# Adding relative distances to attention scores: the strided side moved from the SBUF operand to PSUM

## The chip, the cores and the metric

One core of a Trainium2 chip runs the whole program. The metric is the device time of one execution in microseconds, the median of several runs.

## What is computed

The program runs six blocks one after the other on x (32 sequences of 64 tokens, width 128): cross attention, linear attention with an MLP, an attention mixture, a second cross attention, relative attention, and a causal attention with a mixture of experts. The change concerns only the fifth, with 16 heads of 8 numbers, here cut to its core:

```python
idx = r[None, :] - r[:, None] + (MAX_LEN - 1)
rel = rel_emb[idx]
qk = jnp.einsum('bhld,bhrd->bhlr', q, k) / np.sqrt(HEAD_DIM)
qk = qk + jnp.einsum('bhld,lrd->bhlr', q, rel)
att = jax.nn.softmax(qk, axis=-1)
out = jnp.einsum('bhlr,bhrd->bhld', att, v)
```

The second term of `qk` is the "distances" term: for each query, head and key one number that depends on how far key and query are apart.

## The kernel before

Everything is f32. `stage_relative` works on 16 tiles of 128 rows (two sequences of 64 queries each). A tile's scores are 128 rows by 1024 columns: 16 heads by 64 keys, head outermost. They lie in two PSUM banks, `psS[t % 2]`, columns 0 to 511 (heads 0 to 7) and 512 to 1023 (heads 8 to 15). Two such pairs of banks alternate.

First part of the stage: the distances of all tiles are multiplied out (`distances`, L1746), copied to SBUF (`Z`) and stored to HBM (`hbm_dist`), from where each tile is loaded skewed, so that row and key match, into `S2` (L1673). `S2` has four slots and holds for each row four groups i of four heads; within a group the key k is outer and the head h inner: the order is i, k, h. The heads of a key thus lie next to each other, and consecutive keys of one head lie four words apart.

Second part, the tile loop. TensorE's order in one turn is: score(t+1), mix(t-1), oturn(t-2), turn(t), out(t-2). `score` first multiplies heads 0 to 7 of `S2` by the identity into the first bank with start=True (L1756), then adds the products of queries and masked keys (L1763), which start the second bank themselves. `turn` (L1775) transposes the probabilities, `mix` (L1785) multiplies them by the values, `oturn` and `out` (L1796, L1802) turn the result and project it.

VectorE's order is: shift(t), normalise(t-2), finish(t-3). `shift` adds heads 8 to 15 of `S2` to the second bank in place (L1905), takes the maximum over the keys of each head (L1908), and subtracts it while copying to SBUF (L1911). `normalise` is L1919 and L1922, `finish` is L1930. ScalarE does the exponential (L1858) and the copies out of PSUM (L1851, L1865). GpSimd builds the masked keys (L1698). SP issues the loads of `S2`, four to a tile, and waits before a tile's loads (L105, the helper `wait`) until the slot's old content has been used by L1756 and L1905.

mix(t-1) waits until VectorE has normalised tile t-2; turn(t) waits for the exponential of tile t; score(t+2) waits until tile t was shifted.

Of the kernel before, what the change touches and what calls it, by code (L numbers as in the profile page):

```python
# [97 lines left out]
def wait(eng, sem, value):  # L98

    if isinstance(value, int):  # L100
        if value <= 0:
            return
    else:
        assert value.min_val > 0, "a wait in a loop has to be on a count above zero"
    eng.wait_ge(sem, value)  # L105
# [14 lines left out]
def bc(ap, shape):  # L120
    return ap.broadcast_to(shape)
# [1511 lines left out]
def stage_relative(K):  # L1633
# [3 lines left out]
    SPAN, SLOTS5, AHEAD = 96, 8, 4  # L1637
    dist = K.dram("hbm_dist", (TILES, P, SPAN * HEADS))
    with ExitStack() as st:
        s = K.sems(st, "a5_", "const rel bias biasT biasc biasout q k v qout kout vout zr0 zr1 zr2 zr3 zo0 zo1 zo2 zo3 "  # L1640
                              "st0 st1 st2 st3 st4 st5 st6 st7 in0 in1 in2 in3 kin scored biased maxed shifted exped "
                              "turned tcopied mixed recip normed oT oTc wo xsum added")
# [6 lines left out]
        Z, S2 = sb("Z", [P, SLOTS5, 4, SPAN, 4]), sb("S2", [P, AHEAD, 4, S, 4])  # L1649
# [7 lines left out]
        with nc.Block() as block:  # L1657
            @block.sync
            def _(sp):
                def store(t):  # L1660
                    for i in range(4):
                        sp.wait_ge(s[f"zo{i}"], t + 1)
                    sp.dma_start(dist[t, :, :], Z[:, t % SLOTS5, :, :, :].rearrange("p i j h -> p (i j h)")).then_inc(
                        s[f"st{t % SLOTS5}"], 16)

                def load(t):

                    sp.wait_ge(s[f"st{t % SLOTS5}"], 16 * (t // SLOTS5 + 1))
                    wait(sp, s["biased"], t - AHEAD + 1)
                    wait(sp, s["added"], t - AHEAD + 1)  # L1670
                    for c in range(4):
                        at = (t * P + 32 * c) * SPAN * HEADS + 31 * 4
                        sp.dma_start(S2[32 * c:32 * c + 32, t % AHEAD, :, :, :].rearrange("p i k h -> p i (k h)"),  # L1673
                                     bass.AP(dist.tensor, at, [[SPAN * HEADS - 4, 32], [SPAN * 4, 4], [1, S * 4]])).then_inc(
                                         s[f"in{t % AHEAD}"], 16)

                for t in range(TILES):
                    store(t)
                    if 2 <= t < AHEAD + 2:
                        load(t - 2)  # L1680
                for t in range(AHEAD, TILES):
                    load(t)
# [29 lines left out]
            def _(pe):  # L1712
# [37 lines left out]
                def score(t):  # L1750

                    if t >= TILES:
                        return
                    wait(pe, s["shifted"], t - 1)
                    pe.wait_ge(s[f"in{t % AHEAD}"], 64 * (t // AHEAD + 1))
                    pe.matmul(K.psS[t % 2][:, 0:512].rearrange("p (i h k) -> p i h k", i=2, h=4), K.ident,  # L1756
                              S2[:, t % AHEAD, 0:2, :, :].rearrange("p i k h -> p i h k"), start=True, stop=False,
                              skip_group_check=True).then_inc(s["added"], 1)
                    pe.wait_ge(s["kin"], t + 1)
                    for b in range(TB):  # L1760
                        for r in range(2):
                            rows = slice(64 * r, 64 * r + 64)
                            pe.matmul(K.psS[t % 2][64 * b:64 * b + 64, r * 512:(r + 1) * 512],  # L1763
                                      QT[rows, t * P + 64 * b:t * P + 64 * b + 64],
                                      RK[rows, t % 2, b, :, :].rearrange("p h k -> p (h k)"), start=r == 1, stop=True,
                                      skip_group_check=True).then_inc(s["scored"], 1)
# [44 lines left out]
                for i in range(4):  # L1811
                    pe.wait_ge(s[f"zo{i}"], TILES)
                score(0)
                pe.wait_ge(s["const"], 3)
                pe.wait_ge(s["qout"], GROUPS)
                pe.wait_ge(s["kout"], GROUPS)
                pe.wait_ge(s["vout"], GROUPS)
                for t in range(TILES + 2):
                    score(t + 1)
                    mix(t - 1)  # L1820
                    oturn(t - 2)
                    turn(t)
                    out(t - 2)
# [48 lines left out]
            @block.vector  # L1872
            def _(dve):
                def zcopy(t, i):
                    dve.wait_ge(s[f"zr{i}"], 4 * (t + 1))
                    wait(dve, s[f"st{t % SLOTS5}"], 16 * (t // SLOTS5))
                    dve.tensor_copy(Z[:, t % SLOTS5, i, :, :], psZ[i].rearrange("p (j h) -> p j h", h=4)).then_inc(
                        s[f"zo{i}"], 1)

                def values(g):  # L1880
                    dve.wait_ge(s["v"], 2 * (g + 1))
                    dve.wait_ge(s["const"], 3)
                    dst = Vbd[:, g * GT:(g + 1) * GT, :, :, :, 0:HD].rearrange("p t b c h d -> p (t b c) h d")
                    dve.tensor_tensor(dst, bc(psV[g % 2].rearrange("p (x d) -> p x d", d=HD).unsqueeze(2), [P, 64, 2, HD]),
                                      bc(mask2[:, :].unsqueeze(1).unsqueeze(3), [P, 64, 2, HD]), ALU.mult).then_inc(
                                          s["vout"], 1)

                dve.wait_ge(s["biasT"], 2)
                dve.tensor_tensor(boe[:, :], psV[1][:, P:2 * P], row("bo1"), ALU.add).then_inc(s["biasout"], 1)
                for g in range(GROUPS):  # L1890
                    values(g)
                    for t in range(g * GT, (g + 1) * GT):
                        zcopy(t, 1)
                        zcopy(t, 3)

                def shift(t):
                    if t >= TILES:
                        return
                    sc = K.psS[t % 2][:, :].rearrange("p (h k) -> p h k", h=HEADS)
                    pr = Pr[:, t % 2, :].rearrange("p (h k) -> p h k", h=HEADS)  # L1900
                    top = mx[:, t % 2, :]
                    dve.wait_ge(s["scored"], 4 * (t + 1))
                    dve.wait_ge(s[f"in{t % AHEAD}"], 64 * (t // AHEAD + 1))
                    two = K.psS[t % 2][:, 512:1024].rearrange("p (i h k) -> p i h k", i=2, h=4)
                    dve.tensor_tensor(two, two, S2[:, t % AHEAD, 2:4, :, :].rearrange("p i k h -> p i h k"), ALU.add).then_inc(  # L1905
                        s["biased"], 1)
                    dve.wait_ge(s["biased"], t + 1)
                    dve.tensor_reduce(top, sc, AX.X, ALU.max).then_inc(s["maxed"], 1)  # L1908
                    wait(dve, s["turned"], 2 * (t - 1))
                    dve.wait_ge(s["maxed"], t + 1)  # L1910
                    dve.tensor_tensor(pr, sc, bc(top.unsqueeze(2), [P, HEADS, S]), ALU.subtract).then_inc(s["shifted"], 1)  # L1911

                def normalise(t):
                    if not 0 <= t < TILES:
                        return
                    dve.wait_ge(s["mixed"], TB * (t + 1))
                    ps = K.psO[:, 0:144].rearrange("p (c h e) -> p c h e", c=PAIRS, h=2)
                    wait(dve, s["normed"], t)
                    dve.reciprocal(rl[:, :, :], ps[:, :, :, HD]).then_inc(s["recip"], 1)  # L1919
                    dve.wait_ge(s["recip"], t + 1)  # L1920
                    wait(dve, s["oT"], t - 1)
                    dve.tensor_tensor(o[:, t % 2, :].rearrange("p (c h d) -> p c h d", c=PAIRS, h=2), ps[:, :, :, 0:HD],  # L1922
                                      bc(rl[:, :, :].unsqueeze(3), [P, PAIRS, 2, HD]), ALU.mult).then_inc(s["normed"], 1)

                def finish(t):
                    if not 0 <= t < TILES:
                        return
                    dve.wait_ge(s["wo"], t + 1)
                    dve.wait_ge(s["bias"], 1)
                    dve.tensor_tensor(K.X[:, t, :], K.psM[:, P:P + D], K.X[:, t, :], ALU.add).then_inc(s["xsum"], 1)  # L1930

                for t in range(TILES + 3):
                    shift(t)
                    normalise(t - 2)
                    finish(t - 3)
# [631 lines left out]
```

## Time and profile before

| | us |
|---|---|
| median of 3 runs | 1417.56 |
| lowest and highest | 1414.43, 1423.41 |
| the profiled execution | 1416.64 |
| its span on the core | 1414.8 |
| TensorE busy in the span | 1057.9 (75%) |
| VectorE busy | 772.2 (55%) |
| ScalarE busy | 538.9 (38%) |
| GpSimd busy | 504.2 (36%) |

The span is the time from the first to the last instruction in the trace. The relative-attention stage lies between about 927 and 1068 us of it, its tile loop between about 971 and 1066. Starts and durations of single instructions are in the trace; ends of matmuls are modelled, so the time from one start to the next says more than a record's length.

### The profile page before, as it was taken

To read this page: it belongs to the slowest core of one execution; us is meant where nothing else is said; L and a number is where in the kernel's file an instruction comes from. 1 tells how busy PE (TensorE), PEld (TensorE's weight loads), DVE (VectorE), ACT (ScalarE), POOL (GpSimd) and SP (SyncE) were. 2 spreads that over 40 slices of the span, in tenths; PEclk is the share of its full clock that TensorE was granted. 3 is DMA by queue.
4 is the path that set the end of the run, shared out by engine and by line. 5 is a ranking of instruction groups with operands and counts; after the bars stand their busy time and mean duration, and the time that the engine had idled before them with its cause. 6 is when DMAs were issued, how large, how long until landed. Compare 5 with 4: busy or idle time off the path is not lost. (4 is left out here: it accounts for less than half of the span.)

```text
span 1414.8 us, 28237 instructions
## 1 busy us (share of the span) xinstructions
PE 1057.9 (75%) x11356; PEld 756.5 (53%) x11356; DVE 772.2 (55%) x1529; ACT 538.9 (38%) x972; POOL 504.2 (36%) x484
## 2 busy tenths in 40 slices
PE   1899999986655999999995999789991681208940
PEld 0888888864444566666663666533550361106730
DVE  2255555545753677777775588645873683401112
ACT  0355555542231455555561455343440250002210
POOL 1123222322462566666654122141320551260035
PEclk9999999999985899999996799788995795559985
DMA  9000000000001000000000000057412004313314
GB/s 317 1 2 1 1 1 1 1 1 1 1 1 32 2 2 2 2 2 2 2 2 1 1 2 2 1 181 282 105 31 60 2 3 119 91 52 107 116 57 69
DMA packets 47068, 58.67 MB, mean 41 GB/s; under 512 B 3414, under 2 KB 37336, under 8 KB 46552
## 3 DMA queue, kind: packets, MB, share of 16 engines
q1 hardware_dynamic: 44892, 52.68, 12.0%
q0 software_dynamic: 2048, 4.20, 1.6%
q8 instruction: 91, 1.49, 0.4%
q14 instruction: 37, 0.30, 0.1%
HBM read 32.73 MB, written 24.13 MB: 40 GB/s over the span
## 5 line engine op out<-in xcount | busy, mean ns | idle before, releaser
L1165 POOL TENSOR_TENSOR e_RK<-e_Ks,W 128x1024 f32<-128x1024 f32 x64 | 121.1, 1902 | 35.1 <-DVE e_Ks L1363 21.4
L428 POOL TENSOR_TENSOR c_P<-c_P,c_rl 128x1024 f32<-128x1024 f32 x32 | 60.7, 1898 | 141.2 <-DVE c_rl L572 141.2
L1321 ACT COPY e_PT<-probsT 128x512 f32<-128x512 f32 x128 | 68.8, 589 | 109.3 <-PE probsT L1257 109.3
L1388 DVE TENSOR_REDUCE e_mx<-scores 128x16 f32<-128x1024 f32 x64 | 78.4, 1225 | 56.8 <-PE scores L1246 56.8
L266 PE MATMUL scores<-W,n_xn 128*128 128x128 f32 x80 | 22.3, 434 | 96.3 <-DVE n_xn L246 57.5
L1271 PEld LDWEIGHTS mixed<-e_Vbd,e_PT 128*64 128x64 f32 x2048 | 64.9, 138 | 52.3 <-issue 48.7
L569 DVE TENSOR_REDUCE c_rl<-c_P 128x8 f32<-128x1024 f32 x32 | 39.0, 1219 | 81.9 <-ACT c_P L343 81.9
L1391 DVE TENSOR_TENSOR e_P<-scores,e_mx 128x1024 f32<-128x1024 f32 x64 | 78.4, 1225 | 7.3 <-PE probsT L1257 0.5
L465 PEld LDWEIGHTS misc<-c_xs,c_AQ 128*128 128x128 f32 x488 | 62.2, 193 | 34.5 <-issue 33.5
L1257 PE MATMUL probsT<-W,e_P 128*128 128x128 f32 x512 | 69.1, 278 | 9.4 <-ACT e_P L1328 9.4
L1271 PE MATMUL mixed<-e_Vbd,e_PT 128*64 128x18 f32 x2048 | 71.3, 212 | 1.5 <-DVE e_o L1416 1.2
L489 PE MATMUL mixed<-c_PT,c_cs 128*128 128x512 f32 x128 | 68.0, 613 | 4.5 <-ACT c_RT L543 3.1
L1328 ACT ACTIVATE e_P<-e_P 128x1024 f32<-128x1024 f32 x64 | 68.2, 1065 | 3.8 <-DVE e_P L1391 3.4
L2472 POOL DMA_INDIRECT f_got<-hbm_results,f_back x32 | 31.0, 969 | 108.0 <-PEq L2467 98.6
L266 PEld LDWEIGHTS scores<-W,n_xn 128*128 128x128 f32 x80 | 14.9, 224 | 102.1 <-DVE n_xn L246 61.9
L465 PE MATMUL misc<-c_xs,c_AQ 128*128 128x128 f32 x488 | 67.5, 282 | 2.4 <-ACT c_GT L534 1.7
L1246 PE MATMUL scores<-e_RK,e_QT 64*64 64x512 f32 x512 | 67.6, 603 | 0.0
L475 PE MATMUL scores<-ctxT,c_GT 128*128 128x128 f32 x512 | 64.3, 280 | 0.0
L1257 PEld LDWEIGHTS probsT<-W,e_P 128*128 128x128 f32 x512 | 55.6, 141 | 13.5 <-ACT e_P L1328 12.5
L475 PEld LDWEIGHTS scores<-ctxT,c_GT 128*128 128x128 f32 x512 | 60.7, 195 | 2.3 <-issue 2.3
L543 ACT COPY c_RT<-mixed 128x512 f32<-128x512 f32 x64 | 37.5, 587 | 63.9 <-PE mixed L489 63.9
L499 PE MATMUL mixed<-c_VO,c_RT 128*128 128x128 f32 x512 | 60.1, 276 | 2.0 <-ACT c_RT L543 2.0
(326 smaller groups left out, 2491.9 us busy)
## 6 DMA issues: line engine op xcount, KB each, us to landing
hbm_dist<-u_Z SPq DMA_DIRECT2D x16, 768.0 KB, 6.4
u_S<-hbm_dist SPq DMA_DIRECT2D x64, 128.0 KB, 2.8
e_w<-in_w SPq DMA_DIRECT2D x16, 256.0 KB, 3.8
hbm_slots<-r_zero SPq DMA_DIRECT2D x1, 2560.0 KB, 11.2
e_xin<-hbm_slots SPq DMA_DIRECT2D x8, 320.0 KB, 3.7
hbm_results<-e_yo SPq DMA_DIRECT2D x8, 320.0 KB, 2.8
W<-in_wpack SPq DMA_DIRECT2D x1, 2489.0 KB, 12.6
W<-in_wpack SPq DMA_DIRECT2D x1, 2048.0 KB, 8.6
```

The source lines that it names most:

```text
L428: pool.tensor_tensor(pr, pr, bc(rl[:, a.up, :].unsqueeze(2), [P, PAIRS, KEYS]), ALU.mult).then_inc(s["scaled"], 1)
L465: last = pe.matmul(bank[:, (h % 4) * P:(h % 4 + 1) * P], AQ[:, h, :], xs[:, a.par, :], start=True, stop=True)
L475: last = pe.matmul(K.psS[a.up][:, c * KEYS:(c + 1) * KEYS], GT[:, a.par, a.u, 2 * c:2 * c + 2, :].rearrange("p h q -> p (h q)"), K.ctxT[:, ...
L489: pe.matmul(K.psO[:, :], cs[:, a.up, :], at.PT[:, a.up, r * 512:(r + 1) * 512], start=True, stop=True).then_inc(s["read"], 1)
L1165: pool.tensor_tensor(RK[:, n % 2, :, :, :], bc(Ks[:, t % 2, e, :].rearrange("p (b k) -> p b k", b=TB).unsqueeze(2), [P, TB, 8, S]), bc(w(" ...
L1246: pe.matmul(bank(r, b), QT[rows, t % 2, e, 64 * b:64 * b + 64], RK[rows, n % 2, b, :, :].rearrange("p h k -> p (h k)"), start=False, stop= ...
L1257: last = pe.transpose(K.psT[:, c * P:(c + 1) * P], Pr[:, n % 2, c * P:(c + 1) * P], K.ident)
L1271: last = pe.matmul(K.psO[64 * b:64 * b + 64, c * 18:(c + 1) * 18], PT[:, n % 2, c * P + 64 * b:c * P + 64 * b + 64], Vbd[:, t % 2, u, c, b ...
L1321: act.copy(PT[:, n % 2, half * 512:(half + 1) * 512], K.psT[:, half * 512:(half + 1) * 512]).then_inc(s["tcopied"], 1)
L1328: act.activation(Pr[:, n % 2, :], Pr[:, n % 2, :], ACT.Exp, scale=0.5).then_inc(s["exped"], 1)
L1388: dve.tensor_reduce(top, sc, AX.X, ALU.max).then_inc(s["maxed"], 1)
L1391: dve.tensor_tensor(pr, sc, bc(top.unsqueeze(2), [P, HEADS, S]), ALU.subtract).then_inc(s["shifted"], 1)
```

## The change

Both places that read `S2` read it in the order in which it lies (i, k, h). In exchange the PSUM side is walked in that order too: its view goes from "p i h k" to "p i k h", so that consecutive elements are 64 words apart in the bank. The same numbers meet at the same addresses. Counts, waits, semaphores and the loads are as they were.

```diff
@@ -1753,8 +1753,8 @@
                     wait(pe, s["shifted"], t - 1)
                     pe.wait_ge(s[f"in{t % AHEAD}"], 64 * (t // AHEAD + 1))
-                    pe.matmul(K.psS[t % 2][:, 0:512].rearrange("p (i h k) -> p i h k", i=2, h=4), K.ident,
-                              S2[:, t % AHEAD, 0:2, :, :].rearrange("p i k h -> p i h k"), start=True, stop=False,
+                    pe.matmul(K.psS[t % 2][:, 0:512].rearrange("p (i h k) -> p i k h", i=2, h=4), K.ident,
+                              S2[:, t % AHEAD, 0:2, :, :], start=True, stop=False,
                               skip_group_check=True).then_inc(s["added"], 1)
@@ -1901,9 +1901,8 @@
                     dve.wait_ge(s[f"in{t % AHEAD}"], 64 * (t // AHEAD + 1))
-                    two = K.psS[t % 2][:, 512:1024].rearrange("p (i h k) -> p i h k", i=2, h=4)
-                    dve.tensor_tensor(two, two, S2[:, t % AHEAD, 2:4, :, :].rearrange("p i k h -> p i h k"), ALU.add).then_inc(
-                        s["biased"], 1)
+                    two = K.psS[t % 2][:, 512:1024].rearrange("p (i h k) -> p i k h", i=2, h=4)
+                    dve.tensor_tensor(two, two, S2[:, t % AHEAD, 2:4, :, :], ALU.add).then_inc(s["biased"], 1)
                     dve.wait_ge(s["biased"], t + 1)
```

## Rows read from the trace of the kernel before

**Rows 1.** The page, part 1: busy us, share of the span, instructions.
```profile
PE 1057.9 (75%) x11356; PEld 756.5 (53%) x11356; DVE 772.2 (55%) x1529; ACT 538.9 (38%) x972; POOL 504.2 (36%) x484
```
**Rows 2.** Windows: length, busy us of PE, PEld, DVE, ACT, POOL; clock, DMA share, GB/s.
```profile
928.00:933.00 5.00, 5.00 (x36) 2.46 (x38) 0.29 (x1) 1.38 (x2) 2.06 (x3) 0.59 0.01 3
...
970.00:975.00 5.00, 4.04 (x22) 0.60 (x10) 1.02 (x2) 0.76 (x2) 0.00 (x0) 0.81 1.01 417
...
985.00:1053.00 68.00, 68.00 (x707) 35.05 (x708) 54.86 (x78) 30.89 (x51) 22.85 (x12) 1.00 0.30 79
```
**Rows 3.** Timeline, one tile of the loop: start, duration in us, engine, line, idle before.
```profile
1015.88 1.11 PE L1785 MATMUL mixed<-u_Vbd,u_PT 128*64 128x18 f32 x32
1016.09 1.10 DVE L1905 TENSOR_TENSOR scores<-scores,u_S 128x512 f32<-128x512 f32 x1 [0.83 <-PE scores L1763]
...
1017.96 0.39 PE L1802 MATMUL misc<-W,u_oT 128*128 128x128 f32 x2
...
1018.19 1.96 PE L1756 MATMUL scores<-u_S,W 128*128 128x512 f32 x2
1018.56 1.23 DVE L1911 TENSOR_TENSOR u_P<-scores,u_mx 128x1024 f32<-128x1024 f32 x1
...
1019.82 1.06 ACT L1858 ACTIVATE u_P<-u_P 128x1024 f32<-128x1024 f32 x1 [1.02 <-DVE u_P L1911]
1019.98 0.29 DVE L1922 TENSOR_TENSOR u_o<-mixed,u_rl 128x128 f32<-128x128 f32 x1
...
1020.07 1.09 PE L1763 MATMUL scores<-u_RK,u_QT 64*64 64x512 f32 x8
1020.19 0.28 DVE L1930 TENSOR_TENSOR X<-misc,X 128x128 f32<-128x128 f32 x1
...
1021.09 0.59 PE L1785 MATMUL mixed<-u_Vbd,u_PT 128*64 128x18 f32 x14
1021.31 1.11 DVE L1905 TENSOR_TENSOR scores<-scores,u_S 128x512 f32<-128x512 f32 x1 [0.84 <-PE scores L1763]
```
**Rows 4.** Groups in 970:1056: count, busy us, mean ns, idle before them, releaser.
```profile
L1756 PE MATMUL scores<-u_S,W 128*128 128x512 f32 x32 | 31.6, 1077 | 1.0 <-DVE u_Z L1877 1.0
...
L1905 DVE TENSOR_TENSOR scores<-scores,u_S 128x512 f32<-128x512 f32 x16 | 17.6, 1101 | 17.6 <-PE scores L1763 17.6
```
**Rows 5.** Timeline of VectorE: the adds of tile 2 and of tile 15.
```profile
985.12 1.10 DVE L1905 TENSOR_TENSOR scores<-scores,u_S 128x512 f32<-128x512 f32 x1 [2.54 <-PE scores L1763]
...
1052.61 1.09 DVE L1905 TENSOR_TENSOR scores<-scores,u_S 128x512 f32<-128x512 f32 x1 [0.85 <-PE scores L1763]
```
**Rows 6.** Timeline of TensorE: the first tile's identity products.
```profile
971.41 2.02 PE L1756 MATMUL scores<-u_S,W 128*128 128x512 f32 x2 [0.96 <-DVE u_Z L1877]
973.36 1.99 PE L1763 MATMUL scores<-u_RK,u_QT 64*64 64x512 f32 x8
```
**Rows 7.** TensorE in 1340:1360: L2416's records (ns min/median/max), then its timeline.
```profile
L2416 PE MATMUL scores<-e_xT,e_w x16: 272/434/632, 1340.0 to 1353.4; 128*128 128x512 f32 x8, 128*128 128x128 f32 x8
...
1350.27 1.25 PE L2416 MATMUL scores<-e_xT,e_w 128*128 128x512 f32 x4
1351.35 1.25 PE L2416 MATMUL probsT<-e_xT,e_w 128*128 128x512 f32 x4
```
**Rows 8.** Timeline of TensorE, ahead of the distances: contiguous products, lower clock.
```profile
928.55 1.92 PE L1722 MATMUL mixed<-XnT,W 128*128 128x512 f32 x2
930.25 1.91 PE L1724 MATMUL misc<-XnT,W 128*128 128x512 f32 x2
```
**Rows 9.** Groups of VectorE elsewhere: contiguous (L1363), and writes eight words apart (L1048).
```profile
L1363 DVE TENSOR_TENSOR e_QT<-misc,W 128x512 f32<-128x512 f32 x16 | 11.1, 691 | 5.6 <-PE misc L1212 5.6
...
L1048 DVE TENSOR_TENSOR r_less<-f_logits 128x112 f32<-128x112 f32 x1 | 0.4, 351 | 0.0
...
L1048 DVE TENSOR_TENSOR r_less<-f_logits 128x64 f32<-128x64 f32 x1 | 0.3, 259 | 0.0
```
**Rows 10.** Waits of SP's queue in 930:1062: total us, times, longest.
```profile
SPq L105 <- DVE scores L1905: 40.6, 12, 5.0
```

## The prediction

> **What bounds the kernel now.** I read the page first: TensorE is busy 75% of the span [rows 1], but the two edited lines run only in the relative-attention stage, so the whole-span shares say nothing about them. The windows view places that stage's tile loop: in 985 to 1053 us TensorE is busy 68.00 of 68.00 us at a granted clock of 1.00 (its 2.4 GHz level), VectorE 54.86, ScalarE 30.89, GpSimd 22.85 [rows 2]. Full busy time alone proves nothing, since matmul ends are modelled, so I went on to the timeline of one tile [rows 3] and read starts only. The pattern there repeats for tiles 3 to 14. The mixing products start at 1015.88 and again at 1021.09: a tile takes 5.21 us. Its parts, start to start: mixing, the turn of the output and the transposes 2.08, output product 0.23, the two identity products of L1756 1.88 (1018.19 to 1020.07), the score products of L1763 1.02 (1020.07 to 1021.09). No part is followed by a wait.
>
> VectorE, in the same rows, adds at 1016.09, takes the maximum, subtracts, normalises and finishes at 1020.19 + 0.28 = 1020.47, then stands still 0.84 us until the score products end. All of its idle time before L1905, 17.6 us in this stretch, is put down to L1763 [rows 4]. ScalarE's exponential ends at 1020.88 and TensorE wants it only at about 1022.3. So TensorE's own order sets the pace, VectorE is 0.84 us behind, and the identity products are over a third of the tile.
>
> From tile 2's add (985.12) to tile 15's (1052.61) there are 13 intervals of 5.19 us [rows 5].
>
> **The two products.** The change leaves the count of instructions alone: 32 matmul records for 16 tiles [rows 4], two to a tile. Before, the moving operand is read four words apart and the bank is written in one run; afterwards the operand is read in one run, and the bank is written 64 words (256 bytes) apart. The price before: a pair takes 1.88 us at the 1.00 clock [rows 3] and 1.95 us at a clock of 0.81 in the stage's first stretch [rows 2, 6]. Contiguous 128x512 f32 products of the same engine: four instructions of L2416, two of 512 and two of 128 columns (its records are half of each kind), take 1.08 us start to start, 0.84 ns a column, so 0.86 us for two of 512 [rows 7]; such a pair (L1722) takes 1.70 us [rows 8] where the mean clock is 0.59, that is mostly the 1.2 GHz level [rows 2]. The strided read barely cares about the clock (1.95 against 1.88), while the contiguous product follows it; so what is paid today is the operand's read, and the change does remove it.
>
> What a strided write by TensorE costs, no row shows. From below: nothing, a pair of 0.86. From above: the strided read adds 0.94 - 0.43 = 0.51 us to each product; an accumulating bank is both read and written, so I bound it by twice that, 1.45 us a product, 2.90 a pair. I choose near the lower end, a pair of 0.93, for one reason out of the rows: an f32 product puts out a column only every 0.84 ns at the full clock, so a write may take that long before anyone waits. The choice is the weakest point of the forecast.
>
> The Trainium skill ("PSUM — Partial Sum Buffer", Specifications) speaks against this: it gives PSUM 8-byte cachelines and says that any non-contiguous access pattern slows matmuls significantly. No run so far shows it; it is rival 2, priced there from rows.
>
> **The add (L1905).** Before: PSUM read and written in runs, S2 read four words apart, 1.10 us [rows 4]. A 128x512 f32 tensor_tensor with runs on every side, one source in PSUM, takes 0.69 us (L1363), so the stride costs 0.41 us. Strided writes into SBUF cost about the same: L1048 with 112 and with 64 elements takes 351 and 259 ns, 1.92 ns an element [rows 9]; (1.10 - 0.69) / 512 more is 0.80 ns, on top of about 1.04. Afterwards S2 is read in one run, and PSUM is both read and written 64 words apart. No row shows either on VectorE. Below: 0.69 us, no penalty in PSUM. Above: both sides pay 0.41, 1.51 us. I take 1.10, the middle: one penalty goes and about one comes.
>
> The Trainium skill ("Vector Engine (DVE) Microarchitecture Reference", on the SBUF access granule) gives 1.98 ns a column where all three streams hop every element, against 1.05 contiguous, which by its figures is an estimate of 512 x 1.98 = 1.01 us and a fixed part; it measured SBUF, not PSUM, and no row here shows this form.
>
> **Sum.** Three limits to a tile with a pair of 0.93 and an add of 1.10:
> - TensorE's order: 5.21 - 1.88 + 0.93 = 4.26 us.
> - VectorE's order: from its add to the end of its last piece 4.38, less about 0.08, since a piece that waits for nothing starts before its predecessor's record ends (L1930 at 1020.19, L1922 until 1020.27), so 4.30.
> - The ring through both, over two tiles: scores end to add 0.22 (1021.09 to 1021.31), add to the end of normalising (L1922) 4.18, mixing to the next pair 2.31, pair 0.93, scores 1.02: 8.66, so 4.33 a tile.
>
> These three are now within 0.07 us of each other; I take 4.35. VectorE's order takes over from TensorE's, and of the 0.95 us that leave each pair 0.84 arrive. 13 x (5.19 - 4.35) = 10.9 us. Before them, the first tile's pair at the lower clock (1.95 to at least 1.70) gives 0.25, tile 2's, for which VectorE waits in full, 0.95; tile 1's is hidden behind tile 0's softmax. Total 12.1 us.
>
> Nothing else takes it back in my reading: the loads of S2 wait for VectorE's add, 40.6 us over 12 waits on SP's queue [rows 10], so they have spare time and are issued earlier if the add comes earlier; GpSimd's key masks are busy 1.9 of each 5.2 us. The tail has no identity product. The end of the stage feeds the next stage directly, so its time counts in full.
>
> The sum is made against the profiled execution, 1416.64 us (span 1414.8): 1404.5. The median of the three runs is 1417.56, so 1405 on that footing. One per cent is 14.2 us, and a change under it can hardly be told from none, the three runs before being 9 us apart.
>
> **Rivals.**
> 1. VectorE's add changes size. At 0.69 us VectorE's order is 3.89, the ring 4.12, TensorE's 4.26 binds: 13 x 0.93 + 1.2 + two adds on the chain at the ends (0.8) = 14.1, 1403.5. At 1.51 VectorE's order is 4.71: 13 x 0.48 + 1.2 - 0.8 = 6.6, 1411.
> 2. TensorE's strided write is slow and takes the place of the strided read. A tile is 5.19 + (pair - 1.88). At a pair of 1.88 nothing changes, 1417.5. At 2.90: 16 x 1.02 = 16.3, 1434. It makes the kernel slower at all from a pair of 1.88, and by over 1% from 2.77. For it: each write hits another line, and the bank is accumulated into. Against it: the 0.84 ns a column that f32 leaves.
> 3. The write costs part: a pair of 1.4 gives 13 x 0.46 + 0.7, about 6.7 us, 1411.
> 4. VectorE alone eats the gain: its add would have to reach 1.10 + 0.84 = 1.94 us, past both penalties of rows 9; very unlikely.
>
> **Chances.** Pair near contiguous 0.60 (with the add near 1.1: 0.24, near 0.7: 0.20, near 1.5: 0.16); write part-priced 0.12; pair near 1.9 0.10; slower than 1.9 0.18. The likeliest single case is 1405. Faster by over 1% needs the fast add and some luck of measurement, or a larger ring gain than I see: 0.20. Slower by over 1% needs a pair of 2.77 or more: 0.14. The rest 0.66. The range takes the fast-add case with 3 us of spread below it, and the unchanged case with as much above: 1400 to 1421; most of the 0.18 lies outside. The forecast case's own range is 1402 to 1409.
>
> **What would show it.** Right: L1756's pair under 1.0 us start to start, its record near 600 ns, not 1077; VectorE's idle time before L1905 gone from 17.6 to a few us; small gaps on TensorE; a tile near 4.35. If L1756 stays at 1.88 or more, the reading that f32 leaves room for the write is wrong. If L1905 reads 0.7 the PSUM side is free on VectorE and a tile should be 4.26; at 1.5, 4.7. If both are as forecast and the tile stays above 4.5, the ring is mis-summed.

## The result and the profile after

| | before | after |
|---|---|---|
| median, us | 1420.1 (4 runs, 1414.4 to 1423.4) | 1396.71 (4 runs, 1396.3 to 1397.7) |
| profiled execution, us | 1416.64 | 1396.6 |
| span of the trace, us | 1414.8 | 1394.8 |

The ratio is 0.984, 95% interval 0.9804 to 0.9877. Every ratio here is to the kernel before, run in the same rounds; executions in a far slower state (1965 us of one experiment, 2202 us of the kernel before) are left out of them. A second measurement of the changed kernel, among the experiments, gave 0.9887 (0.9835 to 0.9939). Both intervals hold the 1.3% that the stage itself saves, as the table below shows; the forecast was 0.85%, 1405 us, with a range that began at 1400. The medians are 23.4 us apart; the stage explains 18.6 of them. The kernel is faster by over 1%, to which I had given 0.20.

One tile of the loop in the timeline of the changed kernel (start us, duration us, engine, line, idle before); the lines after L1905 stand one lower than before. It answers [rows 3]. The code has one identity matmul a tile on L1756; in f32 each shows as two records, and these two are "the pair":

```profile
995.26 1.11 PE L1785 MATMUL mixed<-u_Vbd,u_PT 128*64 128x18 f32 x32
995.47 0.70 DVE L1905 TENSOR_TENSOR scores<-scores,u_S 128x512 f32<-128x512 f32 x1 [0.30 <-PE scores L1763]
...
997.57 1.02 PE L1756 MATMUL scores<-u_S,W 128*128 128x512 f32 x2
...
998.52 1.09 PE L1763 MATMUL scores<-u_RK,u_QT 64*64 64x512 f32 x8
...
998.96 0.29 DVE L1921 TENSOR_TENSOR u_o<-mixed,u_rl 128x128 f32<-128x128 f32 x1
999.17 0.28 DVE L1929 TENSOR_TENSOR X<-misc,X 128x128 f32<-128x128 f32 x1
999.54 1.11 PE L1785 MATMUL mixed<-u_Vbd,u_PT 128*64 128x18 f32 x32
999.75 0.70 DVE L1905 TENSOR_TENSOR scores<-scores,u_S 128x512 f32<-128x512 f32 x1 [0.31 <-PE scores L1763]
```

The mixing starts at 995.26 and 999.54: a tile takes 4.28 us, not 5.21. The identity pair takes 998.52 - 997.57 = 0.95 us, not 1.88. The add takes 0.70, not 1.10. VectorE still stands idle before its add, 0.31 us where it was 0.84, which speaks for TensorE as the bound; two experiments below settle it. The groups in 960:1050, to set against [rows 4]:

```profile
L1756 PE MATMUL scores<-u_S,W 128*128 128x512 f32 x32 | 16.5, 599 | 1.0 <-DVE u_Z L1877 1.0
L1905 DVE TENSOR_TENSOR scores<-scores,u_S 128x512 f32<-128x512 f32 x16 | 11.2, 699 | 7.7 <-PE scores L1763 7.7
```

Its start, in the same timeline. With [rows 6] in mind, look at the first group of L1763: 1.99 us before, 1.09 here.

```profile
968.75 1.10 PE L1756 MATMUL scores<-u_S,W 128*128 128x512 f32 x2 [0.96 <-DVE u_Z L1877]
969.78 1.09 PE L1763 MATMUL scores<-u_RK,u_QT 64*64 64x512 f32 x8
...
978.50 0.70 DVE L1905 TENSOR_TENSOR scores<-scores,u_S 128x512 f32<-128x512 f32 x1 [1.14 <-PE scores L1763]
...
1033.99 0.70 DVE L1905 TENSOR_TENSOR scores<-scores,u_S 128x512 f32<-128x512 f32 x1 [0.30 <-PE scores L1763]
...
1046.66 0.39 SPq L1964 DMA_DIRECT2D hbm_g<-X  x1
```

These starts cut the stage in three: from the first identity product to tile 2's add (start), from there to tile 15's add, 13 intervals (loop), and from there to the store that follows the stage (tail). For the kernel before the third mark is 1067.93. The same marks in every trace of this study, in us:

| kernel | start | loop | per tile | tail | sum |
|---|---|---|---|---|---|
| before | 13.71 | 67.49 | 5.19 | 15.32 | 96.52 |
| before again | 13.71 | 67.48 | 5.19 | 15.24 | 96.43 |
| only VectorE's half | 13.32 | 67.49 | 5.19 | 13.11 | 93.92 |
| only TensorE's half | 10.12 | 57.23 | 4.40 | 15.10 | 82.45 |
| after | 9.75 | 55.49 | 4.27 | 12.67 | 77.91 |
| after again | 9.74 | 55.49 | 4.27 | 12.67 | 77.90 |
| identity product twice | 11.46 | 66.46 | 5.11 | 14.61 | 92.53 |
| identity product on 4 columns | 10.13 | 52.34 | 4.03 | 12.66 | 75.13 |
| add on 4 columns | 9.22 | 55.30 | 4.25 | 12.60 | 77.12 |
| bf16 mask products | 9.73 | 55.50 | 4.27 | 14.22 | 79.45 |

The stage saves 18.6 us: 4.0 at the start, 12.0 in the loop, 2.65 in the tail. The other 1.4 us between the two profiled spans lie outside it. The first instruction of the stage (L1715) starts at 927.2 and 932.8 us in the two traces of before, at 924.7 and 924.1 in the two of after, and at 933.1 and 933.3 in two experiments on the changed kernel below: that is spread in a part that the change does not touch. Twelve runs of the kernel before lie 16 us apart; that this spread is the reason was not traced run by run.

### The profile page after: what moved, and what is told of

Read it like the earlier page. It is cut to its first block and busy times, and to the rows that moved or that the text cites. A ratio compares the mean times of both kernels' runs of the same rounds, so it can differ in the third digit from the quotient of the medians.

```text
span 1394.8 us, 28237 instructions
## 1 busy us (share of the span) xinstructions
PE 1040.5 (75%) x11356; PEld 755.1 (54%) x11356; DVE 765.6 (55%) x1529; ACT 538.8 (39%) x972; POOL 503.7 (36%) x484
## 5 line engine op out<-in xcount | busy, mean ns | idle before, releaser
L499 PEld LDWEIGHTS mixed<-c_VO,c_RT 128*128 128x128 f32 x512 | 58.4, 192 | 4.5 <-ACT c_RT L543 4.5
```

The costliest lines, as they stand in the source:

```text
L499: last = pe.matmul(K.psO[:, 0:D], RT[:, a.par, h, :], VO[:, h, :], start=(h == 0), stop=(h == HEADS - 1))
```

## The experiments

The first four ran on one chip, in five rounds.

**The two kernels again.** No edit; they give second traces, above all of the clock.

> The kernel before once more, for a second trace of it. Theory A (the pace of the tensor clock at the stage's two ends is chance): this trace may show the first tiles and the tail at the full clock, and the stretch from the first identity product to tile 2's add is then near 12 us, not 13.71. Theory B (the strided read itself brings the lower clock): it is again 13.5 us or more, with a granted clock near 0.8 in the first 10 us. The 13 intervals between the adds of tiles 2 and 15 are 5.19 us in both. Ratio 1.00.

> The changed kernel once more. Ratio 0.984 as before. Theory A lets the first stretch vary between 9.75 us (full clock) and 11 us or more; theory B has it at 9.7 to 9.8 again, with a clock of 1.00. A tile takes 4.28 us in both.

Measured: 1.0013 (0.9977 to 1.0049) and 0.9887 (0.9835 to 0.9939). The start took 13.71 and 9.74 us, to 0.01 us what it had taken. The granted clock in the first ten microseconds from the first identity product, and the ten after (windows; busy us by engine, then the clock), of the second trace of before:

```profile
977.10:987.10 10.00, 8.22 (x26) 2.48 (x27) 5.78 (x6) 1.10 (x2) 3.80 (x2) 0.76 0.67 240
987.10:997.10 10.00, 10.00 (x101) 5.05 (x100) 6.54 (x8) 4.42 (x7) 3.19 (x2) 0.90 0.38 101
```

and of the second trace of after:

```profile
968.10:978.10 10.00, 7.52 (x52) 2.77 (x54) 6.41 (x7) 3.19 (x4) 3.90 (x3) 1.00 0.85 284
978.10:988.10 10.00, 9.88 (x136) 6.61 (x134) 8.95 (x13) 4.96 (x9) 5.40 (x3) 1.00 0.42 109
```

The first traces read 0.75 and 1.00 in the same ten. So the clock at the start is no chance between traces (theory A falls for the start); what brings it, the next runs narrow down. Shorter windows of the first trace of before show that the mean hides two levels, 1.00 (2.4 GHz) and 0.50 (1.2 GHz):

```profile
971.40:973.00 1.60, 1.58 (x2) 0.28 (x2) 0.00 (x0) 0.00 (x0) 0.00 (x0) 1.00 1.00 410
973.20:976.40 3.20, 3.20 (x11) 0.81 (x10) 0.91 (x1) 0.00 (x0) 0.79 (x1) 0.50 0.79 330
976.60:979.80 3.20, 1.84 (x9) 0.21 (x8) 3.17 (x3) 0.69 (x1) 2.01 (x2) 1.00 0.68 182
980.00:983.20 3.20, 2.98 (x10) 2.10 (x10) 2.51 (x3) 1.73 (x4) 0.61 (x1) 0.50 0.58 159
```

The first identity pair (from 971.41) runs at 1.00 for its first 1.6 us; then the clock falls, and the first score products and the first transposes run at 0.50.

**TensorE's half alone.**

```diff
-                    pe.matmul(K.psS[t % 2][:, 0:512].rearrange("p (i h k) -> p i h k", i=2, h=4), K.ident,
-                              S2[:, t % AHEAD, 0:2, :, :].rearrange("p i k h -> p i h k"), start=True, stop=False,
+                    pe.matmul(K.psS[t % 2][:, 0:512].rearrange("p (i h k) -> p i k h", i=2, h=4), K.ident,
+                              S2[:, t % AHEAD, 0:2, :, :], start=True, stop=False,
```

> Only TensorE's part of the change: the identity product reads in order and writes PSUM 64 words apart; VectorE's add stays as before (1.10 us). By my three limits a tile is 4.35 us (TensorE's order 4.28, VectorE's 4.30, ring 4.33), so this half alone brings nearly all of it: time near 1398, ratio 0.985. Rival: the two halves share the gain because VectorE's order and the ring do not overlap as summed: a tile of 4.5 or more, 1401 or more. By theory B the first stretch is at the full clock here too, and is the changed kernel's plus the 0.4 us of one longer add.

Measured: 0.9933 (0.9901 to 0.9965), median 1407.41. The ratio I expected, 0.985, lies outside; it had been set from the whole change's 0.984, and the stage's 14.1 us are 1.0%. A tile takes 4.40 us in the mean, not 4.35. In the second half of the loop the adds lie alternately 4.5 and 4.3 us apart; two such tiles of the timeline:

```profile
1024.34 1.10 DVE L1905 TENSOR_TENSOR scores<-scores,u_S 128x512 f32<-128x512 f32 x1
...
1028.23 0.29 DVE L1922 TENSOR_TENSOR u_o<-mixed,u_rl 128x128 f32<-128x128 f32 x1
...
1028.66 1.11 DVE L1905 TENSOR_TENSOR scores<-scores,u_S 128x512 f32<-128x512 f32 x1
1028.66 1.11 PE L1785 MATMUL mixed<-u_Vbd,u_PT 128*64 128x18 f32 x32 [0.15 <-DVE u_o L1922]
...
1030.97 1.02 PE L1756 MATMUL scores<-u_S,W 128*128 128x512 f32 x2
...
1033.16 1.09 DVE L1905 TENSOR_TENSOR scores<-scores,u_S 128x512 f32<-128x512 f32 x1
```

The chain goes through both engines: add at 1024.34, normalising until 1028.52, mixing from 1028.66 (TensorE waits for it), pair at 1030.97, score products from 1031.92 to 1032.99, add at 1033.16. That is the ring of the forecast, 8.82 us over two tiles, 4.41 a tile, and it is what bounds this half. TensorE's order (4.28) and VectorE's (4.30) are both shorter. The sum had 8.66: it left out the 0.14 us from the end of normalising to the start of mixing.

**VectorE's half alone.**

```diff
-                    two = K.psS[t % 2][:, 512:1024].rearrange("p (i h k) -> p i h k", i=2, h=4)
-                    dve.tensor_tensor(two, two, S2[:, t % AHEAD, 2:4, :, :].rearrange("p i k h -> p i h k"), ALU.add).then_inc(
-                        s["biased"], 1)
+                    two = K.psS[t % 2][:, 512:1024].rearrange("p (i h k) -> p i k h", i=2, h=4)
+                    dve.tensor_tensor(two, two, S2[:, t % AHEAD, 2:4, :, :], ALU.add).then_inc(s["biased"], 1)
```

> Only VectorE's part: its add reads S2 in order and reads and writes PSUM 64 words apart, 0.70 us a piece; the identity product reads four words apart as before. If TensorE's order sets the pace, a tile stays at 5.19 us, VectorE's idle time before the add grows by 0.4 us a tile, and only two adds at the ends of the loop count: ratio 0.999 to 1.000. If VectorE shared the pace, a tile is 4.9 us or less and the ratio 0.997 or less. By theory B the first stretch is at the lower clock, near 13.3 us.

Measured: 0.9968 (0.9935 to 1.0001), median 1413.5; the interval holds both expectations, so the tile decides. The loop did not move by 0.1 us, while the add fell to 0.70 us. Idle time took its place, by the timeline:

```profile
1051.94 0.70 DVE L1905 TENSOR_TENSOR scores<-scores,u_S 128x512 f32<-128x512 f32 x1 [1.25 <-PE scores L1763]
1057.15 0.70 DVE L1905 TENSOR_TENSOR scores<-scores,u_S 128x512 f32<-128x512 f32 x1 [1.24 <-PE scores L1763]
```

The 2.6 us that the stage saved lie at the ends: 0.39 at the start, which is the shorter add, and 2.2 in the tail (0.4 the shorter add; in the rest the clock differs, see the end of this section). Together with TensorE's half the shorter add is worth 1.7 us more in the loop (57.23 to 55.49), because there it is in the ring.

The next four ran together on one chip, in three rounds, all made from the changed kernel.

**The identity product on 4 columns.** It leaves out nearly all distances of heads 0 to 7.

```diff
-                    pe.matmul(K.psS[t % 2][:, 0:512].rearrange("p (i h k) -> p i k h", i=2, h=4), K.ident,
-                              S2[:, t % AHEAD, 0:2, :, :], start=True, stop=False,
+                    pe.matmul(K.psS[t % 2][:, 0:512].rearrange("p (i h k) -> p i k h", i=2, h=4)[:, 0:1, 0:1, :], K.ident,
+                              S2[:, t % AHEAD, 0:1, 0:1, :], start=True, stop=False,
```

> On the changed kernel, the identity product takes 4 columns instead of 512 (it leaves out nearly all distances of heads 0 to 7). TensorE's order falls by about 0.85 us to 3.4 us a tile, the ring to (8.66 - 0.40 - 0.85) / 2 = 3.7; VectorE's order, 4.30 - 0.40 = 3.90, would be the bound: a tile of 3.90 to 3.95 us, 5 us less over the loop. If TensorE's order was not the bound of the changed kernel, a tile stays at 4.28 us.

Measured: 0.9855 (0.9807 to 0.9902), not to be told apart from after. Most tiles take 3.88 us, the loop 52.3 us (3.1 less than after, not the 5 expected, for its first tiles are slow), and VectorE's idle time before the add is gone:

```profile
1016.54 0.69 DVE L1905 TENSOR_TENSOR scores<-scores,u_S 128x512 f32<-128x512 f32 x1
...
1020.42 0.69 DVE L1905 TENSOR_TENSOR scores<-scores,u_S 128x512 f32<-128x512 f32 x1
```

That is VectorE's order as summed (3.90), the one place where it stands alone. The changed kernel therefore has 0.40 us a tile to win from TensorE before VectorE stops it. The start was a surprise, though: the clock fell further than in the kernel before.

```profile
977.40:987.40 10.00, 7.64 (x38) 3.53 (x38) 6.20 (x6) 3.19 (x4) 3.80 (x2) 0.58 0.83 289
987.40:997.40 10.00, 9.46 (x116) 7.15 (x113) 7.60 (x12) 4.31 (x7) 4.33 (x3) 0.74 0.42 107
```

It stood at 1.00 until 979.0 and at 0.50 from there to 992.7. No operand is read with a stride here. So theory B as I had put it, that the strided read as such brings the lower clock, is too narrow.

**The add on 4 columns.** It leaves out nearly all distances of heads 8 to 15.

```diff
-                    dve.tensor_tensor(two, two, S2[:, t % AHEAD, 2:4, :, :], ALU.add).then_inc(s["biased"], 1)
+                    dve.tensor_tensor(two[:, 0:1, 0:1, :], two[:, 0:1, 0:1, :], S2[:, t % AHEAD, 2:3, 0:1, :], ALU.add).then_inc(s["biased"], 1)
```

> On the changed kernel, VectorE adds 4 columns instead of 512 (it leaves out nearly all distances of heads 8 to 15). If TensorE's order is the bound, a tile stays at 4.28 us and only the ends of the loop gain about 1 us; if VectorE or the ring through both bounds it, a tile is 4.1 us or less and the gain 3 us or more. By theory B (the strided read of TensorE brings the lower clock at the start of the loop) the start is at the full clock.

Measured: 0.9906 (0.9858 to 0.9955).

```profile
1015.38 0.17 DVE L1905 TENSOR_TENSOR scores<-scores,u_S 128x4 f32<-128x4 f32 x1 [0.83 <-PE scores L1763]
...
1019.66 0.17 DVE L1905 TENSOR_TENSOR scores<-scores,u_S 128x4 f32<-128x4 f32 x1 [0.83 <-PE scores L1763]
```

0.53 us less work a tile, 0.52 us more idle time, 4.28 us a tile: TensorE's order bounds the changed kernel, not VectorE and not the ring. The stage gained 0.8 us (77.91 to 77.12), and the clock in the first ten microseconds was 1.00 again, both as expected.

**The identity product twice.** The second overwrites the first, and the output is unchanged.

```diff
+                    pe.matmul(K.psS[t % 2][:, 0:512].rearrange("p (i h k) -> p i k h", i=2, h=4), K.ident,
+                              S2[:, t % AHEAD, 0:2, :, :], start=True, stop=False, skip_group_check=True)
                     pe.matmul(K.psS[t % 2][:, 0:512].rearrange("p (i h k) -> p i k h", i=2, h=4), K.ident,
```

> On the changed kernel, the identity product runs twice, both times reading in order and writing 64 words apart. TensorE then spends about 1.9 us a tile on it, as long as one strided-read pair took before: a tile of 4.28 + 0.95 = 5.23 us, and the whole within 0.3% of the kernel before but for the clock. Theory B: the strided read itself lowers the clock, so here the first score products of L1763 (1.09 us, not 1.99) and the stretch up to tile 2's add run at 1.00. Theory C: any pair of that length lets the clock fall there, since what matters is how late VectorE and ScalarE answer; then the dips to 0.5 come back and L1763's first record is 1.99 us.

Measured: 0.9986 (0.9953 to 1.0018). The timeline prices the pair, and the window shows the clock at the start:

```profile
1016.37 1.02 PE L1756 MATMUL scores<-u_S,W 128*128 128x512 f32 x2
1017.23 1.02 PE L1758 MATMUL scores<-u_S,W 128*128 128x512 f32 x2
1018.18 1.09 PE L1765 MATMUL scores<-u_RK,u_QT 64*64 64x512 f32 x8
```
```profile
977.40:987.40 10.00, 8.36 (x36) 3.28 (x36) 6.21 (x6) 2.57 (x4) 3.80 (x2) 1.00 0.86 299
```

A pair followed by another takes 1017.23 - 1016.37 = 0.86 us, exactly the contiguous price of [rows 7]; followed by the score products, which use the array in 64*64 tiles, 0.95. The strided write is free here. The steady tile is 5.14 us, 0.86 more, not the 0.95 that I expected. And TensorE spends as long on identity products as before (1.81 against 1.88 us), yet the clock stays at 1.00 and L1765 begins at 1.09: theory C, the mere length, falls as well.

Taken together: in all of these traces the clock stood at 1.00 when the first identity product began. It fell 1.5 to 1.7 us later where that product reads with a stride (two of before 0.75 and 0.76 over ten microseconds, VectorE's half 0.76) and where it has 4 columns (0.58). It stayed at 1.00 in all six traces where 512 columns are read in order (two of after, TensorE's half, the add on 4 columns, the product twice, and the bf16 run below). So TensorE's half of the edit is what keeps the clock up, and not by making the pair shorter. What the strided read and the 4 columns have in common was not tested.

**A strided write at bf16's pace.** In the second cross attention the two mask products of 512 columns are bf16. Both now read the mask key by key, each number four times; only the first writes with a stride. The second one's mask lands in wrong places.

```diff
-                    for c in range(2):
-                        pe.matmul(K.psS[n % 2][:, c * 512:(c + 1) * 512].rearrange("p (h k) -> p h k", h=4), identb[:, :],
-                                  bc(neg[:, t, :].unsqueeze(1), [P, 4, KEYS]), start=True, stop=False, skip_group_check=True)
+                    pe.matmul(K.psS[n % 2][:, 0:512].rearrange("p (h k) -> p k h", h=4), identb[:, :],
+                              bc(neg[:, t, :].unsqueeze(2), [P, KEYS, 4]), start=True, stop=False, skip_group_check=True)
+                    pe.matmul(K.psS[n % 2][:, 512:1024].rearrange("p (k h) -> p k h", h=4), identb[:, :],
+                              bc(neg[:, t, :].unsqueeze(2), [P, KEYS, 4]), start=True, stop=False, skip_group_check=True)
```

> On the changed kernel, in the second cross attention the two bf16 mask products of 512 columns (L1494; 379 ns a record, 0.53 us a pair start to start) read the mask key by key, four times each, with the operand's innermost step zero; the first writes PSUM 128 words apart, the second in one run (its mask lands in wrong places, so heads 4 to 7 of each half are masked wrongly). If the strided write is free only because an f32 product gives a column every 0.84 ns, the first one takes up to twice its 0.25 us, a record near 590 ns, and the second stays at 379. If a strided write is free at any pace, both stay at 379. If both grow, the repeated read is what costs.

Measured: 0.9947 (0.9908 to 0.9986), its centre between before and after; the interval overlaps that of after, so the records have to decide. The contiguous write, one line of the experiment's trace (ns, min/median/max):

```profile
L1495 PE MATMUL scores<-x_neg,x_identb x32: 421/421/715, 774.3 to 911.6; 128*128 128x512 bf16 x32
```

the strided write, L1493 in the same trace:

```profile
L1493 PE MATMUL scores<-x_neg,x_identb x32: 592/592/1061, 773.6 to 911.2; 128*128 128x512 bf16 x32
```

and the changed kernel's own, read and write in order:

```profile
L1494 PE MATMUL scores<-x_neg,x_identb x64: 379/379/634, 773.5 to 896.6; 128*128 128x512 bf16 x64
```

By the records the repeated read adds 42 ns and the strided write 171 ns more: 592 ns, which is also what an f32 record of 512 columns shows (599 on average in L1756 after). Starts say the same without the modelled ends. In the experiment:

```profile
839.70 0.59 PE L1493 MATMUL scores<-x_neg,x_identb 128*128 128x512 bf16 x1
840.08 0.42 PE L1495 MATMUL scores<-x_neg,x_identb 128*128 128x512 bf16 x1
840.43 1.09 PE L1501 MATMUL scores<-x_RK,XnT 32*64 32x512 f32 x8
```

and after:

```profile
842.48 0.59 PE L1494 MATMUL scores<-x_neg,x_identb 128*128 128x512 bf16 x2
843.01 1.09 PE L1500 MATMUL scores<-x_RK,XnT 32*64 32x512 f32 x8
```

The pair takes 0.73 us, not 0.53, and 0.38 us of it go by before the second product starts. The second product did not stay at 379 ns, but the first one's growth is mostly the write's. So this strided write is not free at bf16's pace. One gap is left: its stride is 128 words, the relative stage's 64, and no run tried the two strides at one type.

The tail of this kernel's relative-attention stage, whose code there is that of after, took 14.22 us (tile 15's add 1047.64, store 1061.86) and not 12.67; with the product twice, which has the same code in its tail, it took 14.61. The traces with long tails show a lower clock there; that of before:

```profile
1056.00:1068.00 12.00, 7.64 (x81) 6.15 (x81) 2.91 (x11) 3.03 (x6) 0.00 (x0) 0.60 0.01 1
```

and that of after:

```profile
1036.00:1047.00 11.00, 5.37 (x84) 4.22 (x82) 3.85 (x11) 3.63 (x8) 0.00 (x0) 0.92 0.01 1
```

As one code gave all these lengths, 1.5 to 1.9 us of the tail's 2.65 are not safely the change's.

## Why the prediction fell short

**What held.** TensorE's own order is the bound, before and after: VectorE's half alone moved the loop by nothing, and 0.53 us less VectorE work after did not either. The pair was put at 0.93 and took 0.95 (0.86 when another pair follows). The reason given for it was that f32 leaves room for the write; the bf16 run fits that, with the stride as the open point. Rival 2 does not hold for this f32 product. The cacheline rule of the Trainium skill ("PSUM — Partial Sum Buffer", Specifications), that any non-contiguous access pattern slows matmuls significantly, does not hold for it either: 0.86 us a pair is the contiguous price. At bf16 with a stride of 128 words the trace agrees with the rule, 592 ns against 421. All three limits could be seen at work: TensorE's order at 4.28 (4.26 forecast), VectorE's at 3.88 with the identity product on 4 columns (3.90 summed), and the ring at 4.41 in TensorE's half alone, which is the forecast's own case. There the ring had been summed to 4.33 and the tile rounded to 4.35, so the forecast's case would have saved 10.3 us in the loop (67.49 to 57.23), not 10.9.

**The first step that failed: the add.** "I take 1.10, the middle: one penalty goes and about one comes." None came. VectorE read and wrote PSUM 64 words apart in 0.70 us, as long as L1363's instruction, 0.69 [rows 9] (which reads one source as a repeated number, and so was not a run on every side). The SBUF rows on which the upper bound was built do not carry over to PSUM. That was rival 1's first case, with 0.20; its tile of 4.26 came out as 4.27 to 4.28. The shorter add is worth 1.7 us in the loop (57.23 to 55.49). With the 0.6 us that the ring had been summed too short, this leaves the loop 1.1 us above the forecast (12.0 against 10.9).

**The larger one: the start of the loop.** The sum gave it 0.25 + 0.95 = 1.2 us; it saved 4.0, of which the add is 0.4. The kernel that runs the identity product twice starts in 11.46 us at the full clock. From after to it, 1.7 us are the two longer pairs on the path. From it to before, 2.25 us are left: 0.9 in the first score products (1.92 against 1.02) and 0.8 in the first transposes (1.75 against 0.93), both at a clock of 0.50 before, 0.4 in the add, and 0.2 in pairs that are still longer when read with a stride. So the lower clock cost 1.7 us, and the pairs 1.9 where the sum had 1.2.

The starts behind this, of before:

```profile
975.28 2.15 PE L1756 MATMUL scores<-u_S,W 128*128 128x512 f32 x2
...
980.22 1.97 PE L1775 MATMUL probsT<-W,u_P 128*128 128x128 f32 x8 [1.77 <-ACT u_P L1858]
981.97 1.98 PE L1756 MATMUL scores<-u_S,W 128*128 128x512 f32 x2
```

and, with [rows 6] for before's first score products (from 973.36), of the product twice:

```profile
979.35 1.09 PE L1765 MATMUL scores<-u_RK,u_QT 64*64 64x512 f32 x8
980.37 1.13 PE L1756 MATMUL scores<-u_S,W 128*128 128x512 f32 x2
...
984.95 1.09 PE L1777 MATMUL probsT<-W,u_P 128*128 128x128 f32 x8 [1.57 <-ACT u_P L1860]
985.88 1.02 PE L1756 MATMUL scores<-u_S,W 128*128 128x512 f32 x2
```

Two terms failed here. The clock's return had no term at all: I had read the clock [rows 2], and took it as given, though TensorE's half of the edit removes the fall. And the first pair's 0.25 rested on a wrong reading of it. The 0.81 is the mean of 970 to 975 us; the pair itself ran mostly at 1.00, so its contiguous price was 1.03 us, not 1.70, and it gave 0.92 (1.95 to 1.03).

The argument that the strided read barely cares about the clock was made from that same 1.95, but other starts bear it out: a strided product wholly at 0.50 takes 0.91 us (981.97 to 982.88), one at 1.00 takes 0.88 (1018.19 to 1019.07). The sum's 0.94 - 0.43 = 0.51 us for the read compares a pair ahead of the score products with one that has none behind it; like with like it is 0.88 - 0.43 = 0.45.

**The tail.** I gave it nothing, since it has no identity product. The last add is in it, 0.4 us; the rest of the 2.65 us hangs on the clock there, which the runs did not settle as cause or chance.

12.1 forecast, plus 1.1, plus 2.8, plus 2.65, is 18.6 to rounding. The range was too narrow at its lower end for that reason: the price of a clock that may change was in no term and no bound. It also allowed 3 us for measurement where the twelve runs of the kernel before spread over 16 (1409.2 to 1425.1).

## What to carry to other kernels

Where an f32 product needs its operand in another order, try reading in runs and putting the stride on the PSUM side. Here that was free for TensorE, and for VectorE too, while a read four words apart in SBUF doubled TensorE's time and added 0.4 us to VectorE's. A bf16 product paid for a strided write, at 128 words, so price it per type. When an engine's work is shortened, look in short windows at its granted clock in the stretches before it is saturated: here the same edit that shortened the product also kept the clock at 1.00, and that was worth nearly as much at the start. And when several limits lie within 0.1 us, sum the ring with its handovers; one left out, 0.14 us, hid which limit binds.

## What the runs showed of the hardware

- A TensorE write 64 words apart costs an f32 product of 512 columns nothing: 0.86 us a pair of records. A bf16 product with a stride of 128 words takes 592 ns a record, against 421 with the same repeated read and writes in order; start to start the two products take 0.73 us, and 0.53 in the kernel after.
- VectorE reads and writes PSUM 64 words apart in 0.70 us for 512 elements; with PSUM in runs and the SBUF source four words apart it takes 1.10.
- An f32 operand read four words apart takes TensorE 0.88 us a record of 512 columns at a clock of 1.00 and 0.91 at 0.50 (read in order at 1.00: 0.43). Ahead of products on 64*64 tiles a pair takes 0.09 us more (0.95 against 0.86).
- With that read the granted clock was 0.75 to 0.76 in the first ten microseconds of the loop in three of three traces, falling from 1.00 to 0.50 about 1.6 us after the first identity product began. With 512 columns read in order it was 1.00 in six of six; with an identity product of 4 columns 0.58 in the one trace.
